# Curvature flow and two 3x3 convolutions on one core: K is added to the image by an accumulating DMA issued from GpSimd, and the first sum of H's numerator is an accumulating DMA as well

## What is computed

```python
def step(u, _):
    ux, uy, uxx, uxy, uyy = _derivs(u)          # Sobel filters, once and twice
    g2 = ux * ux + uy * uy
    denK = jnp.maximum(1.0 + g2, EPS)
    K = jnp.clip((uxx * uyy - uxy * uxy) / (denK * denK + EPS), -5.0, 5.0)
    denH = jnp.sqrt(1.0 + g2 + EPS)
    H = ((1.0 + uy * uy) * uxx - 2.0 * ux * uy * uxy + (1.0 + ux * ux) * uyy) / (2.0 * denH ** 3 + EPS)
    H = jnp.clip(H, -5.0, 5.0)
    diff = jnp.clip(alpha * K + beta * H, -1.0, 1.0)
    u = u + DT * diff
    u = jnp.pad(u[:, :, 1:-1, 1:-1], ((0, 0), (0, 0), (1, 1), (1, 1)), mode='edge')
    return (u, None)
u, _ = jax.lax.scan(step, x, None, length=10)
x = 0.7 * u + 0.3 * x
out = conv3x3(relu(conv3x3(x, w1) + b1), w2) + b2 + x
```

## Time and profile before

| | us |
|---|---|
| median of 3 runs | 38702.09 |
| lowest and highest run | 38700.71, 38704.57 |
| the profiled execution, its own time | 38698.44 |
| its span in the trace | 38696.7 |
| DVE busy | 34434.0 (89%) |
| PE busy | 34434.2 (89%) |
| ACT busy | 33167.9 (86%) |
| POOL busy | 20465.8 (53%) |
| the SP queue's packets, share of 16 DMA engines' span | 33.5% |
| mean granted TensorE clock | 0.992 |

### The profile page before, as it was taken

How to read it: one execution, slowest core, us unless ns; L and a number is a source line. 1 busy time by engine, 2 the same in 40 slices (tenths; PEclk the granted TensorE clock), 3 DMA queues, 4 the chain that set the end, 5 groups by cost and what they waited for, 6 DMA issues and landing times. The chain is left out here.

```text
span 38696.7 us, 453600 instructions
## 1 busy us (share of the span) xinstructions
PE 34434.2 (89%) x126400; PEld 23294.9 (60%) x126400; DVE 34434.0 (89%) x33108; ACT 33167.9 (86%) x33722; POOL 20465.8 (53%) x7685
## 2 busy tenths in 40 slices
PE   5888888888888888888888888888888888889999
PEld 3666666666666666666666666666666666666666
DVE  8999999999999999999999999999999999993111
ACT  5999999999999999999999999999999999994333
POOL 3555555555555556555555555555555555550000
PEclk9999999999999999999999999999999999999999
DMA  5333333333333333333333333333333333333333
GB/s 189 83 83 82 82 75 78 83 83 82 82 83 83 82 79 74 81 83 83 83 82 83 83 83 76 77 81 83 83 83 82 83 83 80 73 82 83 87 87 85
DMA packets 2687511, 3261.71 MB, mean 84 GB/s; under 512 B 2266180, under 2 KB 2266308, under 8 KB 2364740
## 3 DMA queue, kind: packets, MB, share of 16 engines
q1 hardware_dynamic: 2686276, 3247.70, 33.5%
HBM read 582.33 MB, written 268.44 MB: 22 GB/s over the span
## 5 line engine op out<-in xcount | busy, mean ns | idle before, releaser
L646 PE MATMUL tame_slot<-tame_split,tame_M 128*128 128x512 f32 x51200 | 15156.1, 418 | 4131.5 <-DVE tame_ux L517 3386.6
L646 PEld LDWEIGHTS tame_slot<-tame_split,tame_M 128*128 128x128 f32 x51200 | 9160.8, 190 | 10140.8 <-issue 2690.5
L646 PE MATMUL tame_slot<-tame_halo,tame_M 128*128 128x512 f32 x51200 | 14319.2, 402 | 0.0
L356 POOL TENSOR_TENSOR tame_split<-tame_U,tame_split 128x1024 fp32r<-128x1024 f32 x2560 | 6232.0, 2434 | 12755.0 <-ACT tame_split L391 12755.0
L646 PEld LDWEIGHTS tame_slot<-tame_halo,tame_M 128*128 128x128 f32 x51200 | 9757.9, 191 | 2513.8
L368 POOL TENSOR_TENSOR tame_ux<-tame_ux,tame_cross 128x1024 f32<-128x1024 f32 x2560 | 8071.5, 3153 | 433.4 <-POOL tame_ux L362 433.4
L362 POOL TENSOR_TENSOR tame_ux<-tame_ux,tame_uy 128x1024 f32<-128x1024 f32 x2560 | 6161.8, 2407 | 972.6 <-DVE tame_uy L517 972.6
L431 ACT ACTIVATE tame_slope<-tame_slope 128x2048 f32<-128x2048 f32 x2560 | 4895.4, 1912 | 0.0
L656 PE MATMUL tame_slot<-tame_uxy,tame_unit 128*128 128x512 f32 x10240 | 4810.6, 592 | 5.4 <-DVE tame_slot L540 5.4
L426 ACT ACTIVATE tame_slope<-tame_slope 128x1024 f32<-128x1024 f32 x2560 | 2716.8, 1061 | 2141.4 <-issue 2139.4
L559 DVE TENSOR_TENSOR tame_uyy<-tame_slot,tame_slope 128x1024 f32<-128x1024 f32 x2560 | 3132.2, 1223 | 945.6 <-PE tame_slot L656 938.1
(11 more groups left out here) (74 smaller groups left out, 38207.5 us busy)
## 6 DMA issues: line engine op xcount, KB each, us to landing
tame_halo<-tame_split SPq DMA_DIRECT2D x2560, 520.0 KB
tame_halo<-tame_split SPq DMA_DIRECT2D x2560, 260.0 KB
tame_halo<-tame_split SPq DMA_DIRECT2D x5120, 65.0 KB
tame_U<-in_x SPq DMA_DIRECT2D x256, 512.0 KB, 3.9
tame_stage<-in_x SPq DMA_DIRECT2D x128, 1024.0 KB, 4.9
mixed<-tame_stage SPq DMA_DIRECT2D x128, 1024.0 KB, 6.4
out<-res SPq DMA_DIRECT2D x672, 192.0 KB
xin<-mixed SPq DMA_DIRECT2D x344, 256.0 KB, 4.6
```

The lines of the kernel that those rows point to most:

```text
L356: nc.gpsimd.tensor_tensor(split_rows(c, 1), half_rows(c), split_rows(c, 0).bitcast(F32), ALU.subtract).then_inc(lo_ready, 2)
L646: last = nc.tensor.matmul(ps[name][:, b * BANK:(b + 1) * BANK], M[0:lanes, matrix, :], rows(c, part)[:, b * y:(b + 1) * y, :], start=(n < ...
```

## The change

All in `curvature_flow`:

- K is scaled inside `curvature_k` (a scalar_tensor_tensor that multiplies by alpha*DT and by the inverse, in place in `slope`), `clip_k` clips it at 5 and -5 times alpha*DT (two columns of `par`, in place of immediates), and `add_k` on DVE is gone: POOL issues a DMA that adds `slope[..., 1, :]` to `half(c)` (`accum_op`), 512 KB.
- POOL's tensor_tensor in `second_terms` is gone: POOL issues a DMA that adds `uy2` to `ux2`, 512 KB. `numerator_h` stays a tensor_tensor on POOL, one period later.
- H's product goes to `slope[..., 0, :]`; `curvature_h` and `clip_h` come one period later; `add_h` is `update`, and waits for the K transfer as well.
- `uyy` has one buffer instead of two.
- All engines' orders are changed: PE makes uxx ahead of uxy, and `subtract_square` right behind ux; ACT has square_uxy behind the period's border, and the high part earlier; POOL's `low` comes one period later; SP's halo exchange waits for uxy as the last field.

```diff
-    LAST_FIELD = "uxx"
+    LAST_FIELD = "uxy"
...
-        ux2, uy2, cross, uyy = pair("ux2"), pair("uy2"), pair("cross"), pair("uyy")
+        ux2, uy2, cross = pair("ux2"), pair("uy2"), pair("cross")
+        uyy = sb("uyy", [P, HALF])
...
             def second_terms(t, c):
                 pool.wait_ge(uxx_term, done(t, c))
                 pool.wait_ge(uyy_term, done(t, c))
-                nc.gpsimd.tensor_tensor(ux2[c % 2][:, :], ux2[c % 2][:, :], uy2[c % 2][:, :],
-                                        ALU.add).then_inc(sum_h, 2)
+                pool.sem_inc(terms_taken, 1)
+                pool.dma_start(ux2[c % 2][:, :], uy2[c % 2][:, :], accum_op=ALU.add).then_inc(sum_h[c % 2], 16)
 
             def numerator_h(t, c):
                 pool.wait_ge(cross_term, done(t, c))
-                pool.wait_ge(sum_h, done(t, c))
+                pool.wait_ge(sum_h[c % 2], t * 4 + 16 * (c // 2 + 1))
...
+            def add_k(t, c):
+                pool.wait_ge(k_clipped, done(t, c))
+                pool.sem_inc(k_taken, 1)
+                pool.dma_start(half(c), slope[c % 2][:, 1, :], accum_op=ALU.add).then_inc(k_added[c % 2], 16)
+
             def period(t, k, kind, r):
+                if exists(kind, k - 2):
+                    numerator_h(t, k - 2)
+                if exists(kind, k - 5) and goes_on(kind, k - 5):
+                    low(t, k - 5)
                 if exists(kind, k - 1):
                     second_terms(t, k - 1)
-                    numerator_h(t, k - 1)
-                if exists(kind, k - 4) and goes_on(kind, k - 4):
-                    low(t, k - 4)
+                    if tame:
+                        add_k(t, k - 1)
...
             def square_ux(t, c, fresh):
                 if not fresh:
-                    act.wait_ge(updated, done(t, c - 2))
+                    act.wait_ge(h_ready, done(t, c - 2))
...
             def square_uy(t, c, fresh):
                 act.wait_ge(cross_ready, done(t, c))
                 if not fresh:
-                    act.wait_ge(sum_h, done(t, c - 2))
+                    act.wait_ge(sum_h[c % 2], t * 4 + 16 * (c // 2))
...
+            def copy_uyy(t, c, first):
                 act.wait_ge(ready["uyy"], done(t, c))
+                if not first:
+                    act.wait_ge(prod_k, done(t, c - 1))
...
             def sum_squares(t, c, fresh):
...
-                    dve.wait_ge(inv_h_ready, done(t, c - 2))
+                    dve.wait_ge(updated, done(t, c - 2))
...
             def curvature_k(t, c):
                 dve.wait_ge(num_k_ready, done(t, c))
                 dve.wait_ge(inv_k_ready, done(t, c))
-                nc.vector.tensor_tensor(uyy[c % 2][:, :], ps["uxx"][:, :], slope[c % 2][:, 1, :],
-                                        ALU.mult).then_inc(k_ready, 2)
+                K = slope[c % 2][:, 1, :]
+                stt(K, ps["uxx"][:, :], a_dt, K, ALU.mult, ALU.mult).then_inc(k_ready, 2)
...
+            def clip_k(t, c):
+                K = slope[c % 2][:, 1, :]
+                dve.wait_ge(k_ready, done(t, c))
+                nc.vector.tensor_scalar(K, K, a_top, a_low, ALU.min, ALU.max).then_inc(k_clipped, 2)
...
+            def update(t, c):
+                K, Hh = slope[c % 2][:, 1, :], slope[c % 2][:, 0, :]
+                dve.wait_ge(h_clipped, done(t, c))
                 if tame:
-                    stt(half(c), K, a_dt, half(c), ALU.mult, ALU.add).then_inc(k_added, 2)
...
+                    dve.wait_ge(k_added[c % 2], t * 4 + 16 * (c // 2 + 1))
                     stt(half(c), Hh, b_dt, half(c), ALU.mult, ALU.add).then_inc(updated, 2)
```

97 lines of the change are left out of this document (41 added, 56 removed).

## The result

The changed kernel takes 38426.35 us (median of 4 runs, 38408.96 to 38446.55), the kernel before 38703.21 (4 runs): a ratio of 0.9929 (95% interval 0.9912 to 0.9946). It is faster by 277 us, 0.7%, where 2816 were forecast, and 26 us above the upper end of the range. The profiled execution took 38446.55 us, of which the span is 38444.6.

A forecast was written before the change was run, and what follows sets the result against it. DVE was taken to set the 13.32 us period. Savings of 2350 us in ordinary periods and 466 in last steps, together 2816, off 38698.4 gave 35882 us; the forecast's own range was 35300 to 36500, the range for all reached 38400.

The forecast's parts named there:

- The sign: Whole kernel: the change was expected to make it faster, with chance 0.76; same 0.03, slower 0.21.
- ordinary period, the engines alone: Periods other than a round's last step: ACT at 12.27 us, taken as 12.3, instead of 13.32; 2350 us saved.
- T: Issue to landing of the transfer that makes H's first sum: taken as 4.9 us, ends 3.9 and 13.0.
- K's landing: K's transfer has from `clip_k` to `update` in the next but one period, some 8 us.
- The halo's sum: From `update` to the same place two periods later: 15.5 us plus the landing, which may be 9; no cost.
- the ring: POOL's `numerator_h`, `low`, the sum's transfer, `numerator_h` again: 10 to 10.7 us, hidden below 12.3.
- term for the last step of a round: One period in ten: DVE at 13.1 us, ACT at 13.2, so 13.2 instead of 15.02; 466 us saved.
- The rival of the late halos: Halos land after 10 to 11 us beside accumulating transfers; mean period 13.0 us, 37370 us in all; chance 0.13.
- The rival of the slow transfer: T about 8.6 us, or POOL's issue over 3, makes DVE's 13.32 us 14.1; 40180 us in all; chance 0.21.
- The rival of DVE: DVE stays the bound at about 12.9 us: `clip_k` takes 1.22, POOL holds `clip_h`; 37470 us; chance 0.12.

The follow-up runs named there:

- e5: The changed kernel with both accumulating transfers cut to 64 of 1024 columns, issues, waits and order kept: 36645.49 us.
- e4: The changed kernel with both of GpSimd's transfers as plain copies without addition, same bytes, packets and places: 37100.39 us.
- e12: The changed kernel with only the transfer of H's first sum cut to 64 columns, K's left whole: 37118.40 us.
- e13: The changed kernel with only K's transfer cut to 64 columns, that of H's first sum left whole: 37231.43 us.
- e1: The changed kernel with SP issuing both halves of each halo exchange together, ahead of the edge columns: 39017.89 us.
- e11: e5 with `clip_h` moved between `curvature_k` and `multiply_first` on DVE: 36153.91 us.
- e7: The changed kernel with K added on DVE again, behind `term_uyy`, the sum of H left a transfer: 44973.59 us.

## Why the prediction was wrong

The sign was right, the size was not. Measured and forecast differ by 38426 - 35882 = 2544 us. The terms, each from a difference of two rows of the table:

| term of the sum | forecast | measured | us |
|---|---|---|---|
| ordinary period, the engines alone | 12.3 | 12.49 (e5) | 0.19 x 2048 = 390 |
| traffic in an ordinary period | 0 | 12.79 - 12.49 | 614 |
| traffic at a round change | 0 | 253.1 - 216.1 | 37.0 x 32 = 1184 |
| round change without the traffic | 8 x 12.3 + 8 x 13.2 = 204 | 216.1 (e5) | 12.1 x 32 = 387 |

They add up to 2575, 31 more than the difference. With 20 periods a round change, the two terms of the traffic are 415 and 1376 us.

- **The step that failed** is the treatment of transfers as latencies that are hidden or not, with no term for the time that they take from each other on the shared DMA engines. The prediction put T at 4.9 us by the bytes of other rows, gave K's landing "some 8" us, and said of the halos "I cost it at nothing". An accumulating transfer takes twice a plain one's time on the shared DMA engines (e4); the share went to 0.76, where "perhaps as much again" as 0.33 had been written; and at that share 0.30 us of each ordinary period and 37 us of each round change are lost (e5, e12, e13). K's transfer lands after 6.9 us in the median, and `update` waits for it in 575 of 2310 periods. The halo's sum had 2.4 us for four issues on SP; at 1.21 us each they take 4.8, and in e5, with small transfers, they are back at 0.61. T was 7.0, within its ends of 3.9 and 13.0, and at the edge of the 6.5 to 7.2 given for the ring: `numerator_h` waits in 225 of 2310 periods.
- **What was left out** is the round change's own transfers. The sum has a term for the last step of a round, made of DVE's and ACT's instructions alone (13.2). The loads and the store, whose landings stood in the earlier trace rows, were never asked whether they would still come in time. That is the largest term of the miss, 1184 us.
- **The rival of the late halos** named the right mechanism, sharing with accumulating transfers, and put the mean at 13.0 us. Over all periods it is (12.79 x 2048 + 253.1 x 32) / 2560 = 13.40, and e1 shows that it isn't the halos by themselves. It spread its cost evenly; the halo's part is in the even periods.
- **The rival of the slow transfer** didn't decide: T stayed under 8.
- **The rival of DVE** fell: `clip_k` with columns is 0.81 us, nearer to 0.69 than to 1.22. `clip_h` is 0.07 us longer on average (0.76 against 0.69). What DVE pays for an operation right behind the one it waits for is more than was counted: `clip_h` starts 0.11 us after `curvature_h` ends, and `sum_squares` 0.14 after `update`, where 0.06 was taken (medians of e5).
- **Right**: ACT becomes the bound of the ordinary period where neither the transfers nor DVE's order hold it up (12.27 by the sum of its steps, 12.28 in e11); 12.49 comes from DVE's order, since `clip_h` stands right behind the operation it waits for and `square_uy` waits for what follows, a cost that was booked on DVE, where there was room, and not on ACT. `update` 1.28, blends 1.22, POOL's issues 0.86 and 1.21 us against 1.0.

Open: how much of the 216.1 us of a round change without traffic is the loads' (ACT still waits 158 us for the stage's loads in e5, over some 30 rounds) and how much DVE's and ACT's work; which of the transfers in an even period (the halo's, K's, the sum's) costs how much of it; how much of a round change's loss comes through TensorE's clock; and whether issuing the sum before `low` would help, which wasn't tried.

## What to carry to other kernels

Moving an addition from an engine to an accumulating transfer is paid for on the DMA engines, here at twice what its bytes say, and here everything that was on them paid, the issuing queue included. Before such a change, add up the DMA share in each stage, the rare ones first (here one period in five held all loads and stores), and ask of each transfer that isn't waited for now how much room it has. When a wait for one transfer appears, test whether it is the cause, by moving it or by shrinking the others: in e1 the most visible wait went away and the kernel became slower, and in e7 the longest wait stood on an engine for which the others hardly waited.
